# A residual LSTM and RNN over 512 steps: x*Wx0 by seven block products, and a rearranged step

## Chip, cores and metric

One core of a Trainium2 chip runs the whole kernel. The metric is the device time of one execution in microseconds; before the change it is 2285.53 us, the median of three runs (2284.49 to 2286.43).

## What is computed

```python
# first layer, LSTM: x [16, 512, 512], xW = x @ Wx + b, Wx and Wh [512, 2048]
a = xw_t + prev_h @ Wh
i, f, o = sigmoid(a[:, :H]), sigmoid(a[:, H:2*H]), sigmoid(a[:, 2*H:3*H])
g = tanh(a[:, 3*H:])
next_c = f * prev_c + i * g
next_h = o * tanh(next_c)
# x = x + hs;  second layer, RNN: Wx and Wh [512, 512]
h_next = tanh(h @ Wh + xw_t)
# x = x + hs
```

Everything is fp32. Sixteen sequences go through 512 steps; the second layer takes the first one's output plus x, and starts from the same state cond_1024 as the first.

## The kernel before, in words

The 512 steps run one after another on one core, and five engines have a program each, tied by semaphores. There is no planner: the order of each engine's work is written out by hand in its loop over t, and a wait holds back all that is behind it on the same engine.

**Tiles.** A product has the states as the stationary operand, 128 rows (a quarter of the 512 inputs, index k) by 32 columns, and streams the weights past it. The output has only 32 rows, so each 128-row tile of PSUM is filled by four matmuls side by side, one per quarter q of the array (tiles, L175). A "group" below is such a set of four. The gate columns are laid out so that each half of them holds the i, f, o and g columns of one half of the state.

**Recurrent product of layer one** (recurrent0, L206). The weights are held as two fp16 parts, high and low, and so is the state: the stationary tile holds 16 columns of the state's high part and 16 of its low part. One half of the outputs takes 4 k x 2 parts = 8 groups of 256 columns. The groups of output half 0 come first, and before its third k TensorE waits for the second half of the state (h0_ready[1]). Then come the 8 groups of output half 1.

**x*Wx0** (input0, L191) works on a pair of steps at once, so the stationary tile holds 2 steps x 16 sequences. It is fp32 with 512 columns per matmul, 4 k per pair, two k after each step's recurrent product, one or two steps ahead of their use; an fp32 matmul stands in the trace as two records. ScalarE first puts the bias into the bank (bias0, L470), the product adds to it, and ScalarE copies it, times a mask that picks one of the pair's steps and the scale, into the bank of the recurrent product (seed0, L484), which adds to it.

**Layer two** runs LAG = 4 steps behind: input1 (L218, fp32, 128 columns, two k per step) and recurrent1 (L227, fp16, 8 groups of 128 columns, both weight parts added into the same 128 columns), with bias1 and seed1 on ScalarE. All of it is in one bank, rnn_ps.

**A step on VectorE** (loop at L425): transpose of output half 0 (turn0, L350), add of its high and low rows (add0, L356), the same for half 1, the two products of the gates (gate_products, L362), the cell (cell, L367), the state as an fp16 high part (state_high, L378), as fp32 (L379), and as the low part, the difference (state_low, L386). Between these stand the second layer's parts, turn1 (L400), add1 (L404), state1_high and state1_low (L409, L414), and the outputs add_y0 (L394) and add_y1 (L422). **On ScalarE** (loop at L543): seed0 for the next step, seed1, the second layer's tanh (L555), bias0 or bias1, then gates(0), o_half(0), gates(1), tanh_cell(0), o_half(1), tanh_cell(1) (L502 to L515).

**Queues.** SP loads x in chunks of 16 steps, two buffers, and stores the output per 8 steps; before a load it waits until the first layer and x*Wx0 are through with the buffer. GpSimd works only at the start: memsets, an iota, and an all-reduce over the partitions for the largest weight of each layer (L170), on which VectorE's find_scale (L297) waits. The first layer's scale comes before step 0, the second one's at the end of step 0.

## Time and profile before

| what | value |
|---|---|
| median of three runs | 2285.53 us (2284.49 to 2286.43) |
| the profiled execution | 2284.95 us |
| its span, first to last instruction | 2283.1 us |
| mean granted clock of TensorE | 0.993 of full |
| busy in that span, VectorE | 1976.7 us |
| busy in that span, ScalarE | 1644.5 us |
| HBM traffic | 27.62 MB read, 16.78 MB written |

The profiled execution lies inside the three runs' spread. Its busy times are counted once where instructions of an engine overlap. Matmuls are pipelined, so their durations overlap too, and what a group of them costs is read from one start to the next. In a timeline, "idle before" names who ended the wait.

### The profile page before, as it was taken

How to read it: one execution, taken by the hardware profiler on the slowest of the kernel's cores; microseconds unless marked ns; L12 is line 12 of the kernel's file. 1: busy time of each engine (PE TensorE's matmuls, PEld its weight loads, DVE VectorE, ACT ScalarE, POOL GpSimd, SP SyncE). 2: the span in 40 equal slices, each digit the busy share in tenths (PEclk: the TensorE clock that was granted, in tenths of full speed). 3: DMA queues.
4: the chain of work that ended last, by engine and by line, in shares of the span. 5: the costliest groups of instructions: out<-in, count | busy, mean ns of one | idle time of the engine just before them, and what ended most of it. 6: DMA issues, size and time to landing. Idle time of an engine off the chain costs nothing.

```text
span 2283.1 us, 150617 instructions
## 1 busy us (share of the span) xinstructions
PE 2242.1 (98%) x65564; PEld 1617.7 (71%) x65564; DVE 1976.7 (87%) x10283; ACT 1644.5 (72%) x5662; POOL 1.8 (0%) x10
## 2 busy tenths in 40 slices
PE   5999999999999999999999999999999999999997
PEld 2777777777777777777777777777777777777775
DVE  6888888888888888888888888888888888888887
ACT  5777777777777777777777777777777777777775
POOL 0000000000000000000000000000000000000000
PEclk7999999999999999999999999999999999999999
DMA  5000000000000000000000000000000000000000
GB/s 210 18 13 18 23 23 18 14 18 23 23 18 23 13 18 23 23 18 13 18 23 23 18 23 13 18 23 23 18 13 22 19 23 18 23 14 18 23 13 13
DMA packets 16738, 54.03 MB, mean 24 GB/s; under 512 B 2256, under 2 KB 2384, under 8 KB 14800
## 3 DMA queue, kind: packets, MB, share of 16 engines
q1 hardware_dynamic: 16080, 44.41, 5.5%
q8 instruction: 517, 8.47, 1.6%
q14 instruction: 141, 1.16, 0.2%
HBM read 27.62 MB, written 16.78 MB: 19 GB/s over the span
## 4 chain that ended last, share of the span: by engine, by line
PE 97%; DVE 1%; ACT 1%; DMA 1%; issue 0%; SPq 0%; POOL 0%; DVEq 0%; ACTq 0%
PE rec_ps L178 39%; PE in_ps L178 38%; PE rnn_ps L178 20%; DMA wh_sb<-wh 1%; ACT wh_part L480 0%; DVE wh_part L318 0%; DVE largest_slice L277 0%; DVE turned L350 0%; DVE uv L362 0%; DVE h_parts L378 0%; DVE pre_sb L356 0%; ACT wx_sb L468 0%; DVE turned L400 0%; ACT gates_cell L504 0%; ACT rnn_ps L500 0%
## 5 line engine op out<-in xcount | busy, mean ns | idle before, releaser
L178 PE MATMUL in_ps<-wx_sb,x_sb 128*32 128x512 f32 x8192 | 976.4, 594 | 18.4 <-ACT wx_sb L468 18.4
L178 PE MATMUL rec_ps<-wh_part,h_parts 128*32 128x256 f16 x32704 | 988.9, 273 | 5.3 <-DVE h_parts L386 5.3
L178 PEld LDWEIGHTS rec_ps<-wh_part,h_parts 128*32 128x32 f16 x32704 | 867.4, 97 | 13.1 <-issue 8.0
L350 DVE STREAM_TRANSPOSE turned<-rec_ps 128x256 f32<-128x256 f32 x1024 | 461.0, 450 | 196.7 <-PE rec_ps L178 151.5
L178 PEld LDWEIGHTS in_ps<-wx_sb,x_sb 128*32 128x32 f32 x8192 | 259.0, 110 | 327.7 <-issue 319.1
L178 PEld LDWEIGHTS rnn_ps<-wx_sb,y 128*32 128x32 f32 x8192 | 247.0, 110 | 302.5 <-issue 301.0
L490 ACT ACTIVATE rec_ps<-in_ps,mask_scaled 128x256 f32<-128x256 f32 x1022 | 406.6, 435 | 0.4 <-issue 0.2
L178 PE MATMUL rnn_ps<-wh_part,h_parts 128*32 128x128 f16 x16352 | 323.9, 219 | 7.9 <-DVE h_parts L414 7.9
L178 PE MATMUL rnn_ps<-wx_sb,y 128*32 128x128 f32 x8192 | 318.5, 273 | 1.3 <-ACT rnn_ps L500 1.3
L504 ACT ACTIVATE gates_cell<-gate_ps,unscale 128x128 f32<-128x128 f32 x511 | 187.9, 368 | 180.7 <-DVE gate_ps L356 180.7
L500 ACT ACTIVATE rnn_ps<-rnn_ps,mask_scaled 128x128 f32<-128x128 f32 x511 | 174.8, 342 | 188.7 <-DVE turned L400 188.5
L178 PEld LDWEIGHTS rnn_ps<-wh_part,h_parts 128*32 128x32 f16 x16352 | 287.9, 97 | 9.3 <-ACT rnn_ps L500 5.6
L504 ACT ACTIVATE gates_cell<-pre_sb,unscale 128x128 f32<-128x128 f32 x511 | 205.3, 402 | 119.8 <-DVE pre_sb L356 119.8
L509 ACT ACTIVATE o_scaled<-gates_cell 128x32 f32<-128x32 f32 x1024 | 226.7, 221 | 16.3
L362 DVE SCALAR_TENSOR_TENSOR uv<-gates_cell 128x64 f32<-128x64 f32 x1024 | 227.4, 222 | 1.8 <-ACT gates_cell L504 1.3
L367 DVE SCALAR_TENSOR_TENSOR gates_cell<-uv 128x32 f32<-128x32 f32 x1024 | 196.6, 192 | 35.1
L386 DVE TENSOR_TENSOR h_parts<-h_full,h_parts 128x32 f16<-128x32 f32 x1024 | 192.6, 188 | 18.8
L514 ACT ACTIVATE tanh_c_sb<-gates_cell 128x32 f32<-128x32 f32 x512 | 117.5, 229 | 106.5 <-DVE gates_cell L367 106.3
L555 ACT ACTIVATE h_full<-pre,unscale 128x64 f32<-128x64 f32 x511 | 172.3, 337 | 2.3 <-DVE pre L404 2.3
L400 DVE STREAM_TRANSPOSE turned<-rnn_ps 128x128 f32<-128x128 f32 x512 | 162.3, 317 | 12.6 <-PE rnn_ps L178 4.1
L356 DVE TENSOR_TENSOR gate_ps<-turned 128x128 f32<-128x128 f32 x512 | 153.6, 300 | 17.6
L471 ACT ACTIVATE in_ps<-b_sb 128x512 f32<-128x512 f32 x256 | 151.1, 591 | 0.1
(52 smaller groups left out, 1276.0 us busy)
## 6 DMA issues: line engine op xcount, KB each, us to landing
x_sb<-xT SPq DMA_DIRECT2D x32, 512.0 KB, 3.8
yT<-y SPq DMA_DIRECT2D x64, 256.0 KB, 2.0
wh_sb<-wh SPq DMA_DIRECT2D x5, 1024.0 KB, 9.7
wx_sb<-wx SPq DMA_DIRECT2D x5, 1024.0 KB, 14.4
b_sb<-b SPq DMA_DIRECT2D x1, 256.0 KB, 2.7
b_sb<-b SPq DMA_DIRECT2D x1, 64.0 KB, 12.2
h_first<-h0T SPq DMA_DIRECT2D x1, 32.0 KB, 11.6
```

Of the source, the lines that this page charges most:

```text
L178: last = nc.tensor.matmul(out[QUAD * q:QUAD * (q + 1)], states, weights(q), start=False, stop=True, tile_position=(0, QUAD * q), skip_grou ...
L350: nc.vector.transpose(turned0[:, half].rearrange("p b n -> p (b n)"), rec0_ps[t % 2][half][:, 0:COLSH]).then_inc(turned0_done[half], 1)
L356: nc.vector.tensor_tensor(slices(pre0[half]), turned0[:, half, :, 0:BATCH], turned0[:, half, :, BATCH:], ALU.add).then_inc(pre0_done[half], 1)
L362: nc.vector.scalar_tensor_tensor(uv[:, half], gates_cell[:, half, 0:2], 1.0, gates_cell[:, half, 3:5], ALU.add, ALU.mult).then_inc(uv_done ...
L367: nc.vector.scalar_tensor_tensor(gates_cell[:, half, GATES], uv[:, half, 1], 0.5, uv[:, half, 0], ALU.mult, ALU.add).then_inc(cell_done[ha ...
L386: nc.vector.tensor_tensor(h0_parts[:, subs, BATCH:], slices(h0_full[:, cols]), h0_parts[:, subs, 0:BATCH], ALU.subtract).then_inc(h0_ready ...
L400: nc.vector.transpose(turned1[:, :].rearrange("p b n -> p (b n)"), rec1_ps).then_inc(turned1_done, 1)
L490: last = nc.scalar.activation(rec0_ps[t % 2][half][:, 0:COLSH], in0_ps[t // PAIR % 2][:, half * COLSH:(half + 1) * COLSH], ACT.Copy, scale ...
L500: nc.scalar.activation(rec1_ps, in1_ps[s // PAIR % 2], ACT.Copy, scale=own).then_inc(seed1_done, 1)
L504: nc.scalar.activation(gates_cell[:, half, 0:GATES].rearrange("p g n -> p (g n)"), pre0[half], ACT.Tanh, scale=unscale[0][:, :] if t else ...
L509: nc.scalar.activation(o_scaled[:, half], gates_cell[:, half, 2], ACT.Copy, bias=H_SCALE / 2, scale=H_SCALE / 2).then_inc(o_scaled_done[ha ...
L555: nc.scalar.activation(h1_full[:, :], pre1[:, :], ACT.Tanh, scale=unscale[1][:, :] if s > 1 else 1.0).then_inc(h1_full_done, 1)
```

## The change

**x*Wx0 by seven block products.** The unit is now a span of four steps, two pairs. x is cut into a pair (first or second) and a half of k, Wx0 into a half of k and a half of the columns: 2 x 2 blocks times 2 x 2 blocks, eight block products of 2 k by 256 columns. They are replaced by seven over sums of blocks (units). GpSimd forms four sums of the blocks of Wx0 once, at the start (sum_wx0, 2048 columns each), and four sums of the blocks of x per chunk of 16 steps (sum_x, 256 columns each), one at each of the steps 3 to 6 of the chunk before. The first span is done by eight plain block products. The 14 units of a span (7 products x 2 k) are spread over four steps as 4, 3, 4 and 3. Results shared by several blocks are copied on: ScalarE copies v to SBUF (copy_v) and z to c11 (begin_c11), and VectorE adds z and v into c12 (begin_c12) and at the end of the span into c22 (finish_c22); biases go into z and v, each 256 columns wide.

**Layer two's recurrent product** keeps the two weight parts apart: four groups of 256 columns, high and low part side by side. seed1 writes half of the seed into both. Afterwards ScalarE copies the low part's 128 columns to SBUF (copy_low1), VectorE adds the high part's (sum1), and the transpose reads that sum from SBUF. input1 is split into three k and one k over two steps.

**The order.** One group of output half 1 (k = 0, high part) stands before the wait for the state's second half. The second output half has one bank instead of two. On VectorE, sum1, the new adds and turn1 stand ahead of turn0(0); high parts, cells and low parts of the state are reordered; add_y1 stands before state_low(1). On ScalarE, seed0 is issued by half, tanh1 is behind gates(0). find_scale and the weight parts of layer two come two steps later. The start and the loads are adapted.

```diff
+    def sum_x(v, i):
...
+        x = x_sb[:, v % 2].rearrange("p k (g r t) n -> p r k g (t n)", g=PER_CHUNK, r=2)
+        a11, a12, a21, a22 = x[:, 0, 0:SUBH], x[:, 0, SUBH:SUB], x[:, 1, 0:SUBH], x[:, 1, SUBH:SUB]
+        sums = x_sums[:, v % 2]
+        if i == 0:
+            pool.wait_ge(x_in[v % 2], loads(v))
+            if v >= 2:
+                pool.wait_ge(slot_done, slots_until((v - 1) * CHUNK - 6))
+        if i in (1, 3):
+            pool.wait_ge(x_summed, 4 * v + i)
+        out, one, op, other = ((sums[:, 0], a21, ALU.add, a22), (sums[:, 1], sums[:, 0], ALU.subtract, a11),
+                               (sums[:, 2], a11, ALU.subtract, a21), (sums[:, 3], a12, ALU.subtract, sums[:, 1]))[i]
+        nc.gpsimd.tensor_tensor(out, one, other, op).then_inc(x_summed, 1)
...
+    def sum_wx0(i):
+        b11, b12 = wx0_sb[:, 0:SUBH, :, 0:COLSH], wx0_sb[:, 0:SUBH, :, COLSH:COLS]
+        b21, b22 = wx0_sb[:, SUBH:SUB, :, 0:COLSH], wx0_sb[:, SUBH:SUB, :, COLSH:COLS]
+        if i < 2:
+            pool.wait_ge(wx0_doubled, SUBH * (i + 1))
+        if i in (1, 3):
+            pool.wait_ge(wx0_summed, i)
+        one, other = ((b12, b11), (b22, wx0_sums[:, 0]), (b22, b12), (b21, wx0_sums[:, 1]))[i]
+        nc.gpsimd.tensor_tensor(wx0_sums[:, i], one, other, ALU.subtract).then_inc(wx0_summed, 1)
...
+    reduce_largest(0)
+    for i in range(4):
+        sum_wx0(i)
+    reduce_largest(1)
+    for t in range(STEPS):
+        v, c = divmod(t, CHUNK)
+        if 3 <= c < 7 and v + 1 < CHUNKS:
+            pool.wait_ge(rec0_done[0], t + 1)
+            sum_x(v + 1, c - 3)
...
+    def units(g, first, end):
+        z = z_ps[g % 2]
+        products = (
+            (z, lambda k: x_pair(g, 0, k), wx0_block(0, 0)),
+            (v_ps[g % 2], lambda k: x_sum(g, 0, k), wx0_sum(0)),
+            (z, lambda k: x_sum(g, 1, k), wx0_sum(1)),
+            (c11_ps, lambda k: x_pair(g, 0, SUBH + k), wx0_block(1, 0)),
+            (z, lambda k: x_sum(g, 2, k), wx0_sum(2)),
+            (c12_ps, lambda k: x_sum(g, 3, k), wx0_block(1, 1)),
+            (z, lambda k: x_pair(g, 1, SUBH + k), wx0_sum(3)),
+        )
+        sum_of = {1: 0, 2: 1, 4: 2, 5: 3}
+        for u in range(first, end):
+            j, k = divmod(u, 2)
+            if k == 0:
+                if j == 0 and g % PER_CHUNK == 0:
+                    pe.wait_ge(x_in[g // PER_CHUNK % 2], loads(g // PER_CHUNK))
+                if j in sum_of:
+                    sums_ready(g, sum_of[j])
+            out, states, weights = products[j]
+            last = tiles(out, states(k), lambda q: weights(k, q))
+        last.then_inc(slot_done, 1)
...
+    def recurrent0(t):
+        def group(half, k, part):
             cols = slice(half * COLSH, (half + 1) * COLSH)
-            for k in range(SUB):
-                if t and half == 0 and k % SUBH == 0:
-                    pe.wait_ge(h0_ready[k // SUBH], t)
-                for part in weights:
-                    last = tiles(rec0_ps[t % 2][half][:, 0:COLSH], states[:, k], lambda q: part[:, k, q, cols])
-            last.then_inc(rec0_done[half], 1)
+            return tiles(rec0_ps(t, half), h0_parts[:, k], lambda q: wh0_part[part][:, k, q, cols])
+        pe.wait_ge(seed0_done[0], t + 1)
+        pe.wait_ge(h0_ready[0], t)
+        for k in range(SUBH):
+            for part in range(2):
+                group(0, k, part)
+        pe.wait_ge(seed0_done[1], t + 1)
+        group(1, 0, 0)
+        pe.wait_ge(h0_ready[1], t)
+        for k in range(SUBH, SUB):
+            for part in range(2):
+                last = group(0, k, part)
+        last.then_inc(rec0_done[0], 1)
+        for k in range(SUB):
+            for part in range(0 if k else 1, 2):
+                last = group(1, k, part)
+        last.then_inc(rec0_done[1], 1)
...
-        for k in range(half * SUBH, (half + 1) * SUBH):
+        for k in (range(SUB - 1, SUB) if half else range(SUB - 1)):
             last = tiles(in1_ps[r % 2], y0[:, r % Y0_PAIRS, k].rearrange("p t n -> p (t n)"), lambda q: wx1_sb[:, k, q])
...
-    def recurrent1(s, states, weights):
+    def recurrent1(s):
...
         for k in range(SUB):
-            for part in weights:
-                last = tiles(rec1_ps, states[:, k], lambda q: part[:, k, q])
+            if s:
+                last = tiles(rec1_ps, h1_parts[:, k], lambda q: wh1_parts[:, k, q].rearrange("p b w c -> p (b w c)"))
+            else:
+                last = tiles(rec1_by_part[:, :, 0], h_first[:, k], lambda q: wh1_sb[:, k, q])
         last.then_inc(rec1_done, 1)
...
             if t == 1:
                 pe.wait_ge(w_low, 1)
-            recurrent0(t, h0_parts, wh0_part)
-            p, half = divmod(t + 3, PAIR)
-            if p < PAIRS:
-                input0(p, half)
+            recurrent0(t)
+            if t < SLOTS:
+                g, part = divmod(t + 5, SPAN)
+                pe.wait_ge(seed0_done[0], t + 2)
+                if part == 0:
+                    pe.wait_ge(z_biased, g - 1)
+                elif part == 1:
+                    pe.wait_ge(c11_begun, g)
+                elif part == 2:
+                    pe.wait_ge(c12_begun, g)
+                else:
+                    pe.wait_ge(c22_done, g)
+                    if g + 1 < SPANS:
+                        pe.wait_ge(v_biased, g)
+                units(g, UNITS_OF_PART[part], UNITS_OF_PART[part + 1])
         s = t - LAG
         if s >= 0:
...
+    def begin_c12(g, t):
+        dve.wait_ge(slot_done, slots_until(t - 1))
+        dve.wait_ge(v_copied, g)
+        dve.wait_ge(seed0_done[1], t + 1)
+        nc.vector.tensor_tensor(c12_ps, z_ps[g % 2], v_sb[:, :], ALU.add).then_inc(c12_begun, 1)
+    def finish_c22(g, t):
+        dve.wait_ge(slot_done, slots_until(t - 1))
+        if g >= 2:
+            dve.wait_ge(seed0_done[1], SPAN * (g - 1))
+        nc.vector.tensor_tensor(c22_sb[g % 2][:, :], z_ps[g % 2], v_sb[:, :], ALU.add).then_inc(c22_done, 1)
...
+    def sum1(s):
+        dve.wait_ge(rec1_copied, s + 1)
+        nc.vector.tensor_tensor(rec1_sum[:, :, :], rec1_by_part[:, :, 0], rec1_low[:, :, :],
+                                ALU.add).then_inc(rec1_summed, 1)
     def turn1(s):
-        dve.wait_ge(rec1_done, s + 1)
-        nc.vector.transpose(turned1[:, :].rearrange("p b n -> p (b n)"), rec1_ps).then_inc(turned1_done, 1)
+        dve.wait_ge(rec1_summed, s + 1)
...
     for t in range(END):
-        n, s = t + 1, t - LAG
-        lstm, rnn, rnn_state = t < STEPS, 0 <= s < STEPS, s >= 1
-        if lstm:
-            if t == 0:
-                rnn_largest()
-                dve.wait_ge(cell_zeroed, 1)
-            turn0(0, t)
-            add0(0, n)
-            turn0(1, t)
-        if rnn_state:
-            state1_high(s - 1)
-        if lstm:
-            add0(1, n)
-            gate_products(0, n)
-            cell(0, n)
-        if rnn_state:
-            state1_low(s - 1)
-        if lstm:
-            gate_products(1, n)
-            cell(1, n)
-            state_high(0, n)
-        if rnn_state:
-            add_y1(s - 1)
-        if lstm:
-            state_low(0, n)
-            state_high(1, n)
-            state_low(1, n)
+        n, s = t + 1, t - LAG - 1
+        lstm, rnn = t < STEPS, s >= 0
+        g, part = divmod(t + 5, SPAN)
+        if t == 0:
+            rnn_largest()
+            dve.wait_ge(cell_zeroed, 1)
+        if rnn:
+            sum1(s)
+        if lstm and t < SLOTS:
+            if part == 2:
+                begin_c12(g, t)
+            elif part == 3:
+                finish_c22(g, t)
         if rnn:
             turn1(s)
         if lstm:
-            add_y0(t)
+            turn0(0, t)
         if rnn:
             add1(s)
-        if t == 0:
-            find_scale(1, 7)
-        elif t == 1:
+        if lstm:
+            add0(0, n)
+            turn0(1, t)
+            add0(1, n)
+            gate_products(0, n)
+        if rnn:
+            state1_high(s)
+        if lstm:
+            cell(0, n)
+        if rnn:
+            state1_low(s)
+        if lstm:
+            gate_products(1, n)
+            state_high(0, n)
+            cell(1, n)
+            state_full(0, n)
+            state_low(0, n)
+            state_high(1, n)
+            state_full(1, n)
+        if rnn:
+            add_y1(s)
+        if lstm:
+            state_low(1, n)
+            add_y0(t)
+        if t == 2:
+            find_scale(1, done + 1)
+        elif t == 3:
...
+    def bias_z(g):
+        return nc.scalar.activation(z_ps[g % 2], b0_sb[:, 0:COLSH], ACT.Copy)
+    def bias_v(g):
+        return nc.scalar.activation(v_ps[g % 2], b0_diff[:, :], ACT.Copy)
+    def copy_v(g):
+        if g >= 2:
+            act.wait_ge(c22_done, g - 1)
+        nc.scalar.activation(v_sb[:, :], v_ps[g % 2], ACT.Copy).then_inc(v_copied, 1)
+    def begin_c11(g):
+        return nc.scalar.activation(c11_ps, z_ps[g % 2], ACT.Copy)
...
-    def seed0(t):
-        act.wait_ge(in0_done, t // PAIR + 1)
-        if t >= 2:
-            for half in range(HALVES):
-                act.wait_ge(turned0_done[half], t - 1)
+    def seed0(half, t):
+        g, part = divmod(t, SPAN)
+        source = ((c11_ps, c12_ps) if part < PAIR else (z_ps[g % 2], c22_sb[g % 2][:, :]))[half]
+        if half == 0 and t >= 2:
+            act.wait_ge(turned0_done[0], t - 1)
+        if half == 1 and t >= 1:
+            act.wait_ge(turned0_done[1], t)
         own = (mask_scaled[0] if t else mask)[:, t % PAIR:t % PAIR + 1]
-        for half in range(HALVES):
-            last = nc.scalar.activation(rec0_ps[t % 2][half][:, 0:COLSH], in0_ps[t // PAIR % 2][:, half * COLSH:(half + 1) * COLSH],
-                                        ACT.Copy, scale=own)
-        last.then_inc(seed0_done, 1)
+        return nc.scalar.activation(rec0_ps(t, half), source, ACT.Copy, scale=own).then_inc(seed0_done[half], 1)
+    def in1_by_part(i):
+        return in1_ps[i].rearrange("p (b w c) -> p b w c", w=1, c=QUAD).broadcast_to([P, SUB, 2, QUAD])
     def seed1(s):
         act.wait_ge(in1_done, s // PAIR + 1)
         if s:
-            act.wait_ge(turned1_done, s)
-        own = (mask_scaled[1] if s else mask)[:, s % PAIR:s % PAIR + 1]
-        nc.scalar.activation(rec1_ps, in1_ps[s // PAIR % 2], ACT.Copy, scale=own).then_inc(seed1_done, 1)
+            act.wait_ge(rec1_summed, s)
+        own = (mask_scaled[1] if s else mask_half)[:, s % PAIR:s % PAIR + 1]
+        nc.scalar.activation(rec1_by_part, in1_by_part(s // PAIR % 2), ACT.Copy, scale=own).then_inc(seed1_done, 1)
+    def copy_low1(s):
+        act.wait_ge(rec1_done, s + 1)
+        nc.scalar.activation(rec1_low[:, :, :], rec1_by_part[:, :, 1], ACT.Copy).then_inc(rec1_copied, 1)
+    def tanh1(s):
+        act.wait_ge(pre1_done, s + 1)
+        nc.scalar.activation(h1_full[:, :], pre1[:, :], ACT.Tanh,
+                             scale=unscale[1][:, :] if s else 1.0).then_inc(h1_full_done, 1)
...
     for t in range(END):
         s = t - LAG
-        if t + 1 < STEPS:
-            seed0(t + 1)
-        if t == 1:
+        g, part = divmod(t + 5, SPAN)
+        ahead = t < SLOTS
+        if t < STEPS:
+            act.wait_ge(slot_done, slots_until(t - 1))
+            if t:
+                seed0(1, t)
+        if s >= 1:
+            copy_low1(s - 1)
+        if t < STEPS:
+            if t + 1 < STEPS:
+                seed0(0, t + 1)
+            if t == 1:
+                copy_v(1)
+            if part == 0 and g < SPANS:
+                act.wait_ge(seed0_done[0], t + 2)
+                bias_z(g).then_inc(z_biased, 1)
+            elif part == 1 and ahead:
+                act.wait_ge(seed0_done[0], t + 2)
+                if g > 1:
+                    copy_v(g)
+                begin_c11(g).then_inc(c11_begun, 1)
+            elif part == 3 and g + 1 < SPANS:
+                bias_v(g + 1).then_inc(v_biased, 1)
+        if t == 3:
             act.wait_ge(scaled, 2)
             for k in range(SUB):
-                high_part(flat(wh1_sb[:, k]), 1, flat(wh1_part[0][:, k]))
+                high_part(wh1_sb[:, k].rearrange("p q (b c) -> p (q b) c", c=QUAD), 1,
+                          wh1_parts[:, k, :, :, 0].rearrange("p q b c -> p (q b) c"))
         if 0 <= s < STEPS:
             seed1(s)
+        if t < STEPS:
+            gates(0, t)
         if s >= 1:
-            act.wait_ge(pre1_done, s)
-            nc.scalar.activation(h1_full[:, :], pre1[:, :], ACT.Tanh,
-                                 scale=unscale[1][:, :] if s > 1 else 1.0).then_inc(h1_full_done, 1)
-        if t % 2 == 0 and t // 2 + 2 < PAIRS:
-            act.wait_ge(seed0_done, t + 2)
-            bias0(t // 2 + 2)
```

## Rows read from the trace of the kernel before

**Rows 1.** The page, part 1: busy time, share of the span, instructions.

```profile
PE 2242.1 (98%) x65564; PEld 1617.7 (71%) x65564; DVE 1976.7 (87%) x10283; ACT 1644.5 (72%) x5662; POOL 1.8 (0%) x10
```

**Rows 2.** Table by stretch, whole loop: busy per engine, granted clock, DMA share, GB/s.

```profile
100.00:2200.00 2100.00, 2099.96 (x61778) 1521.96 (x61771) 1835.35 (x9653) 1531.76 (x5308) 0.00 (x0) 1.00 0.06 19
```

**Rows 3.** Timeline of TensorE in mid-run: start us, duration us, instruction, [idle before].

```profile
1001.17 0.62 PE L178 MATMUL rnn_ps<-wx_sb,y 128*32 128x128 f32 x16
1001.61 0.63 PE L178 MATMUL rnn_ps<-wh_part,h_parts 128*32 128x128 f16 x32
1002.05 1.94 PE L178 MATMUL rec_ps<-wh_part,h_parts 128*32 128x256 f16 x64
1003.80 1.90 PE L178 MATMUL in_ps<-wx_sb,x_sb 128*32 128x512 f32 x16
1005.51 0.62 PE L178 MATMUL rnn_ps<-wx_sb,y 128*32 128x128 f32 x16
...
1006.40 1.94 PE L178 MATMUL rec_ps<-wh_part,h_parts 128*32 128x256 f16 x64
```

**Rows 4.** Timeline of VectorE and ScalarE, same stretch: two waits.

```profile
1007.50 0.45 DVE L350 STREAM_TRANSPOSE turned<-rec_ps 128x256 f32<-128x256 f32 x1 [0.30 <-PE rec_ps L178]
...
1003.98 0.37 ACT L504 ACTIVATE gates_cell<-gate_ps,unscale 128x128 f32<-128x128 f32 x1 [0.51 <-DVE gate_ps L356]
```

**Rows 5.** Timeline of all engines near the end, steps without x*Wx0.

```profile
2260.08 1.93 PE L178 MATMUL rec_ps<-wh_part,h_parts 128*32 128x256 f16 x64 [0.32 <-DVE h_parts L386]
...
2262.06 0.45 DVE L350 STREAM_TRANSPOSE turned<-rec_ps 128x256 f32<-128x256 f32 x1
...
2262.55 0.29 DVE L356 TENSOR_TENSOR pre_sb<-turned 128x128 f32<-128x128 f32 x1
...
2262.87 0.40 ACT L504 ACTIVATE gates_cell<-pre_sb,unscale 128x128 f32<-128x128 f32 x1 [0.24 <-DVE pre_sb L356]
...
2263.31 0.23 DVE L362 SCALAR_TENSOR_TENSOR uv<-gates_cell 128x64 f32<-128x64 f32 x1
...
2263.57 0.19 DVE L367 SCALAR_TENSOR_TENSOR gates_cell<-uv 128x32 f32<-128x32 f32 x1
...
2263.77 0.18 DVE L379 TENSOR_TENSOR h_full<-o_scaled,gate_ps 128x32 f32<-128x32 f32 x1
2263.79 0.23 ACT L514 ACTIVATE tanh_c_sb<-gates_cell 128x32 f32<-128x32 f32 x1 [0.21 <-DVE gates_cell L367]
...
2264.01 0.18 DVE L386 TENSOR_TENSOR h_parts<-h_full,h_parts 128x32 f16<-128x32 f32 x1
...
2264.23 0.19 DVE L379 TENSOR_TENSOR h_full<-o_scaled,tanh_c_sb 128x32 f32<-128x32 f32 x1
...
2264.34 1.93 PE L178 MATMUL rec_ps<-wh_part,h_parts 128*32 128x256 f16 x64 [0.32 <-DVE h_parts L386]
2264.45 0.19 DVE L386 TENSOR_TENSOR h_parts<-h_full,h_parts 128x32 f16<-128x32 f32 x1
```

**Rows 6.** Timeline of TensorE: step 6, and a second-layer step behind the last state.

```profile
66.36 1.93 PE L178 MATMUL rec_ps<-wh_part,h_parts 128*32 128x256 f16 x64
...
2272.83 0.63 PE L178 MATMUL rnn_ps<-wh_part,h_parts 128*32 128x128 f16 x32 [1.69 <-DVE h_parts L414]
```

**Rows 7.** Groups of instructions by line, whole run: busy us, mean ns, idle before.

```profile
L490 ACT ACTIVATE rec_ps<-in_ps,mask_scaled 128x256 f32<-128x256 f32 x1022 | 406.6, 435 | 0.4 <-issue 0.2
...
L500 ACT ACTIVATE rnn_ps<-rnn_ps,mask_scaled 128x128 f32<-128x128 f32 x511 | 174.8, 342 | 188.7 <-DVE turned L400 188.5
...
L356 DVE TENSOR_TENSOR gate_ps<-turned 128x128 f32<-128x128 f32 x512 | 153.6, 300 | 17.6
```

**Rows 8.** Timeline of GpSimd, first 45 us.

```profile
0.72 0.53 POOL L164 MEMSET zeros<- 128x512 f16 x1 [0.29 <-POOLq L604]
...
11.73 0.13 POOL L167 IOTA partition<- 128x1 int32 x1 [10.25 <-issue]
21.56 0.38 POOL L170 PARTITION_ALL_REDUCE largest_all<-largest  x1 [9.70 <-issue]
38.69 0.35 POOL L170 PARTITION_ALL_REDUCE largest_all<-largest  x1 [16.75 <-DVE largest L277]
```

155 lines of the change are left out of this document (105 added, 50 removed).

## The prediction

> **What bounds the kernel now.** I read the page first: TensorE is busy for 98% of the span, VectorE for 87%, ScalarE for 72% and GpSimd does nothing [rows 1]. Busy shares do not say which of these ends a step, so the next view is the table by stretch: between 100 and 2200 us TensorE is busy all the time and its granted clock is 1.00, the 2.4 GHz level [rows 2]. Then one step of the timeline [rows 3]. From one start of the first layer's recurrent product to the next is 1006.40 - 1002.05 = 4.35 us, and inside it stand 1.75 us of recurrent product, 1.71 us of x*Wx0 (1003.80 to 1005.51), and, a step earlier, 0.44 us of the second layer's input product (1001.17 to 1001.61) and 0.44 us of its recurrent one (to 1002.05). Nothing is left over: a step is TensorE's work. The other engines say the same by waiting: VectorE idles 0.30 us for the product before it transposes, ScalarE 0.51 us before the gates [rows 4].
>
> How far is the next bound? The last steps show it, because there x*Wx0 has run out and TensorE waits 0.32 us for the state. Two recurrent products start 4.26 us apart there (2260.08, 2264.34) [rows 5]. So the chain product, transpose, add, gates, cell, tanh, state takes 4.26 us by itself. **Only 0.09 us of a saving on TensorE would be kept if that chain stayed as it is.** Over the whole loop, step 6 starts at 66.36 us and step 511 at 2264.34: 2197.98 / 505 = 4.352 us a step [rows 5, 6].
>
> **TensorE's new step.** Sixteen groups of four matmuls with 256 fp16 columns take 1.75 us, 0.109 us each. x*Wx0 streams 512 fp32 columns in 4 record groups in 1.71 us, 0.43 us each, so it is paid by the column. Per four steps it had 16 such groups, 6.86 us; seven block products instead of eight leave 7/8 of the columns, plus about 0.03 us for twice as many starts: 6.03 us, 1.51 us a step, 0.43 us for each of the 14 units (one k of one product, two passes of 256 columns). That saves 0.21 us a step. The second layer's recurrent product turns eight groups of 128 columns into four of 256: the same columns, 0.44 us for both; I give it nothing. The input product is split 3 + 1 over two steps instead of 2 + 2, which evens out the 3 and 4 units of x*Wx0 beside it. TensorE's step becomes 4.352 - 0.21 = **4.14 us**.
>
> **The chain's new step.** I count from R, the start of the groups that need the state's second half. Before, 12 groups follow R (1.31 us), then 0.23 us until the transpose of half 1. From that transpose [rows 5]: add +0.49, gates +0.81, products +1.25, cell +1.51, tanh +1.73, second state (L379) +2.17, its low part +2.39 to +2.58, and TensorE starts 0.15 us after a low part is written (64.01 + 0.18 to 64.34). 1.31 + 0.23 + 2.58 + 0.15 = 4.27, and the rows show 4.26: the count holds. Now the moved group: 11 groups follow R, 0.11 us less. VectorE also reaches the second state sooner, since one of the queued operations ahead of it goes: 0.06 us. That path is 4.08 us. The other path goes through the first half: cell 1, then h_full 0, then the low part of half 0 at R + 3.26, written at 3.45, TensorE at 3.60; but now five groups (four and the moved one) stand before the next R: 3.60 + 0.545 = **4.145 us**. So TensorE's work and the chain come out level, and both are 0.21 us shorter than the step now. Whatever delays either is paid in full.
>
> **What is put into the chain.** On VectorE each step now begins with sum1, which waits for ScalarE's copy, which waits for TensorE's last product. TensorE's product ends 0.545 us before R; +0.25 for the wait, +0.30 for the copy (not shown: between 0.23 for 32 columns, L514, and 0.342 for the 128-column activation with a pointer scale [rows 5, 7]; I take it near the latter), so sum1 starts at R + 0.02. It is an add of 128 columns, 0.300 us [rows 7]. Behind it the second layer's transpose, moved from after the state to here, starts at R + 0.36 and lets go of VectorE at 0.60; the first transpose of layer one is due at R + 0.68 and does not wait. Of this 0.00 is on the path. In two steps of four an add of 256 columns (0.300 + 128 more columns, about 0.43) stands between them. In the first (begin_c12) transpose 0 slips to 0.81, add0(0) to 1.29, transpose 1 to 1.50 instead of 1.43: 0.07 us. After that late step sum1 comes 0.07 us early against R, and the second (finish_c22) costs nothing.
>
> On ScalarE the worst step is the one with copy_v and begin_c11: copy_low1 at R - 0.31, seed0 at -0.07, both done at 0.37, copy_v, then begin_c11 ready at about R + 1.15 to 1.24, while TensorE wants it at R + 1.20: 0.03 us late. A seed is 0.435 us [rows 7], and two overlap by 0.07. Behind it seed1, now writing 256 columns, ends its issue at R + 1.45; gates(0) are due at 1.50. bias_z and bias_v take the place of bias0 and hide in the 0.51 us gap [rows 4]. Together 0.10 us in four steps, 0.025 us a step: **4.17 us**.
>
> **GpSimd in the loop** is new: four sums of 256 columns in every 16 steps, each released by rec0_done[0], at R + 0.7. No row shows GpSimd beside VectorE. The bounds: nothing, or all of the delay worked out under the first rival, 0.08 us a step. It could not gain anything, as it only adds work. I take 0.02, nearer to nothing, since it reaches add1 alone and the two transposes read PSUM. That gives **4.19 us** a step.
>
> **Moved or rewired at no cost.** add_y1 now stands between h_full 1 and its low part, in the 0.22 us that this pair waits for each other anyway (2264.23 to 2264.45) [rows 5]. The second half's bank is single now: seed0(1) is issued behind tanh_cell(1), done at R - 0.42, and TensorE wants it at R - 0.11 for the moved group; if that cover went, each 0.1 us would be a step's. SP's wait before an x load changes its semaphore only: the load is issued some 11 steps before its first use and lands in microseconds. The second layer's state must be back for its product at R + 3.15; the chain transpose 1 at 0.36, add1 1.05, tanh1 1.78, state1 low 2.7 is there before. VectorE's queue itself is no bound: its 87% of 2283 us are 3.86 us a step with overlaps counted once, and sum1 and a half of a 256-column add bring about 0.4 more; where this fills the step is inside the path above.
>
> **The start** gets longer. GpSimd shows 10.25 us of issue before its IOTA, 9.70 before the first all-reduce and none before the second [rows 8]: I read this as about 10 us for each change between kinds of operation. tensor_tensor after the all-reduce, the all-reduce again, and the sums after it are three more. The all-reduce would come at about 28 us behind the sums over x instead of at 21.56, then 10 of change to 38; four sums over 2048 columns, at between one and three passes of the memset's rate (0.53 us for 512 columns [rows 8]), 2.1 to 6.3 us each; I take 4.2, because two inputs are read: 55; 10 of change; the second all-reduce at 65, which VectorE awaits at the end of step 2. Step 4 starts near 69.5, step 6 near 78: **+12 us** against 66.36 [rows 6]. If changes cost far less with the loads over, +3; at the dear end +20. **The end**: the steps behind the last state wait only for their own chain (TensorE idles 1.69 us in one [rows 6]), which gains a copy and an add, 0.7 us in each of four: +3 us.
>
> By the Trainium skill (GPSIMD Engine Reference, Performance versus the Vector engine) a tensor_tensor of 2048 fp32 elements takes 4497 ns on GpSimd; with it the start would be +13 instead of +12.
>
> **The sum**: 505 x (4.352 - 4.19) = -82; +12; +3: -67 on a span of 2283.1 gives 2216. The profiled execution took 2284.95, 1.85 us more than its span, and the median of the runs is 0.6 above that: **2218.5 us**, 2.9% faster.
>
> **Rivals.**
> 1. **GpSimd's sum holds VectorE's two-input operations off.** A sum of 256 columns lasts between 0.3 us (one pass at the memset's rate) and 0.94 (three); take 0.62. It starts at R + 0.78 and ends at 1.40. add1, with both inputs in SBUF, could start at 1.05, so add0(0) comes at 1.52, transpose 1 at 1.73 instead of 1.43: 0.30 us in 4 of 16 steps, 0.075 us a step. 4.245: 2247 us. For it: the place is in the chain. Against it: no row. Chance 0.22. The Trainium skill (SBUF — State Buffer, Who interferes with whom) says that a VectorE instruction with two SBUF inputs contends with a GpSimd instruction that reads SBUF; no run here shows it yet.
> 2. **ScalarE's run of copies is late.** If copy_low1, copy_v and begin_c11 each cost 0.1 us more than assumed, c11 is 0.3 us later once in four steps, 0.075 us a step: 2247 us too. Chance 0.15.
> 3. **Nothing added is on the path**: 4.145 us and a start of +7: 505 x 0.207 = 104.5 less 10: 2191 us. Chance 0.12.
> 4. **Slower**: the mechanism of rival 1, with sums that last over 0.93 us. Then each costs over 0.61 us, a step exceeds 4.32, and the 15 us at both ends are no longer covered. At 1.2 us: 0.88 x 4/16 = 0.22, a step of 4.39, 2320 us. The upper bound of a pass count, 0.94, just reaches the point. Chance 0.06.
>
> **Numbers.** The forecast has 0.45. The range takes in rivals 1 to 3 and the ends' bounds (3 to 20 us at the start): 2190 to 2260. A measurement can tell about 0.2%, 4.6 us, from no change. Faster 0.92, same 0.02, slower 0.06.
>
> **What would show it.** Right: recurrent products about 4.17 to 4.19 us apart; x*Wx0 1.51 us of each step; TensorE over 98% busy, or idle only before the recurrent product or before the unit after begin_c11; transposes 1.42 us after R. GpSimd shows two more issue gaps near 10 us before 66 us. Rival 1: add1 longer or later in steps 3 to 6 of every 16. Wrong: steps over 4.3 us, a transpose 0 that waits for sum1 in every step, or x*Wx0 that costs more than 0.43 us per unit of 256 columns.

## The result, and the profile after

The changed kernel takes 2291.20 us (median of 12 runs, 2287.06 to 2296.74) against 2285.62 for the kernel before (12 runs): a ratio of 1.0025, 95% interval 1.0017 to 1.0033. It is slower by a quarter of a per cent, where 2218.5 us were forecast. The profiled execution took 2291.07 us with a span of 2289.3. Part 1 of its page, against [rows 1]:

```profile
PE 2205.7 (96%) x63548; PEld 1838.2 (80%) x63548; DVE 2118.7 (93%) x11050; ACT 1776.5 (78%) x6431; POOL 115.7 (5%) x143
```

TensorE is busy for 36 us less than before, and the span is 6 us longer: the engine now waits. To see where, I take the start of the transpose of half 1 as the mark of a step. In the kernel before the 7th stands at 68.34 us and the 512th at 2266.32, 4.352 us a step; after, at 92.29 and 2268.56, 4.309 a step. So 505 steps gained 21.7 us where 82 were forecast, the way to the 7th grew by 24.0 us where 12 were, and the rest behind the last by 4.0 where 3 was.

**The steps alternate.** The timeline of TensorE after, against [rows 3]:

```profile
1002.65 0.62 PE L244 MATMUL c_ps<-wx_sb,x_sums 128*32 128x256 f32 x8
1003.26 0.43 PE L244 MATMUL rnn_ps<-wx_sb,y 128*32 128x128 f32 x8
...
1006.96 0.87 PE L244 MATMUL rnn_ps<-wx_sb,y 128*32 128x128 f32 x24
1007.61 0.65 PE L244 MATMUL rnn_ps<-wh_parts,h_parts 128*32 128x256 f16 x16
...
1010.69 1.05 PE L244 MATMUL in_ps<-wx_sums,x_sums 128*32 128x256 f32 x16
1011.73 0.43 PE L244 MATMUL rnn_ps<-wx_sb,y 128*32 128x128 f32 x8
```

and of ScalarE in the same stretch:

```profile
1002.41 0.40 ACT L704 ACTIVATE gates_cell<-pre_sb,unscale 128x128 f32<-128x128 f32 x1
1002.76 0.20 ACT L714 ACTIVATE gate_ps<-gates_cell 128x32 f32<-128x32 f32 x1
1002.90 0.26 ACT L663 ACTIVATE rnn_ps<-b_sb 128x128 f32<-128x128 f32 x1
```

The unit that starts at 1002.65 costs 0.43 us everywhere else, but the one quarter of the second layer's input product behind it starts only at 1003.26, 0.61 later. In front of it TensorE's program waits for in1_biased: the bias copy L663 runs at 1002.90 to 1003.16, behind the gates and the tanh of the cell. Two steps later the same (16 records take 1.04 instead of 0.86 before 1011.73). The step between (1006.96) has no such wait. The bias waited for is not that of the quarter part behind it: it is the next pair's, which the three-quarter part reads a step later. The wait stands so early in both kernels; what the change moved is the copy on ScalarE, from in front of gates(0) to behind tanh_cell(0). So odd steps take 4.32 us and even ones 4.15. The table of waits does not name ScalarE for it; it has it as issue time of the weight loads (us in total, times, longest), once in every second step:

```profile
PEld rnn_ps L244 <- issue: 142.2, 272, 2.7
```

**Steps with a sum on GpSimd.** In four steps of every 16 the period is 0.21 us longer. Timelines of GpSimd and VectorE in one of them, and then the same VectorE line in a step without a sum:

```profile
1457.65 0.73 POOL L211 TENSOR_TENSOR x_sums<-x_sb 128x256 f32<-128x256 f32 x1 [55.36 <-PE rec_first_ps L244]
```

```profile
1457.98 0.48 DVE L572 TENSOR_TENSOR pre<-turned 128x64 f32<-128x64 f32 x1
...
1001.23 0.18 DVE L572 TENSOR_TENSOR pre<-turned 128x64 f32<-128x64 f32 x1
```

add1, a 64-column add with both inputs in SBUF, lasts 0.48 us instead of 0.18 and ends at 1458.46, just behind the sum (1458.38). add0 and the transpose of half 1 stand behind it. This is rival 1 of the prediction, in its place and with nearly its size. By the rule that the prediction named with it (the Trainium skill, SBUF — State Buffer, Who interferes with whom), the trace agrees.

**The start.** GpSimd's first 61 us, against [rows 8]:

```profile
1.77 0.14 POOL L192 IOTA partition<- 128x1 int32 x1 [0.29 <-issue]
...
17.34 0.72 POOL L211 TENSOR_TENSOR x_sums<-x_sb,x_sums 128x256 f32<-128x256 f32 x1
26.89 0.38 POOL L195 PARTITION_ALL_REDUCE largest_all<-largest  x1 [8.84 <-issue]
...
35.41 4.60 POOL L222 TENSOR_TENSOR wx_sums<-wx_sb 128x2048 f32<-128x2048 f32 x1 [8.15 <-issue]
...
49.98 4.82 POOL L222 TENSOR_TENSOR wx_sums<-wx_sb,wx_sums 128x2048 f32<-128x2048 f32 x1
...
60.78 0.38 POOL L195 PARTITION_ALL_REDUCE largest_all<-largest  x1 [5.98 <-DVE largest L418]
```

and VectorE beside the four large sums:

```profile
32.42 1.42 DVE L463 SCALAR_TENSOR_TENSOR wh_part<-wh_sb,w_scale,wh_part 128x512 f16<-128x512 f32 x2 [0.33 <-ACT wh_part L669]
34.17 23.83 DVE L463 SCALAR_TENSOR_TENSOR wh_part<-wh_sb,w_scale,wh_part 128x512 f16<-128x512 f32 x10 [0.33 <-ACT wh_part L669]
```

Two low parts of the weights take 1.42 us alone; the next ten take 23.83 instead of some 7. Taken one by one, four of the ten last 5.0 to 5.1 us, each until just behind the end of one of GpSimd's four sums of 4.6 to 5.0 us, and the other six 0.74 us. The changes of GpSimd's kind of operation cost 8.84 and 8.15 us, and the third, in front of the second all-reduce, at most 5.98, where the forecast had about 10 for each. So that all-reduce comes at 60.78, before the 65 of the forecast; late are VectorE's low parts.

**Rare long steps.** Beside the three patterns there are single steps of 4.6 to 5.3 us, in which TensorE's rows fall into pieces of one to four quarters. Above the medians of their place in the 16 they come to about 12 us in the loop (between 1 and 3 before, by how the medians are rounded). What they are is read from the traces behind e14.

The step adds up: 4.15, and 252 x 0.17 / 505 = 0.085 for the bias, 124 x 0.21 / 505 = 0.052 for the sums, 12.3 / 505 = 0.024 for the rare ones: 4.31, measured 4.309. The last term is only what is left over. The experiments take the others away one at a time, then ask what made the 4.15.

### The profile page after: what moved, and what is told of

Read it like the earlier page. It is cut to its first block, busy times and chain, and to the rows that moved or that the text cites. A ratio compares the mean times of both kernels' runs of the same rounds, so it can differ in the third digit from the quotient of the medians.

```text
span 2289.3 us, 148190 instructions
## 1 busy us (share of the span) xinstructions
PE 2205.7 (96%) x63548; PEld 1838.2 (80%) x63548; DVE 2118.7 (93%) x11050; ACT 1776.5 (78%) x6431; POOL 115.7 (5%) x143
## 4 chain that ended last, share of the span: by engine, by line
PE 95%; DVE 2%; issue 1%; ACT 1%; DMA 1%; POOL 0%; SPq 0%; DVEq 0%; ACTq 0%; POOLq 0%
PE in_ps L244 24%; PE rnn_ps L244 22%; PE rec_first_ps L244 20%; PE rec_second_ps L244 19%; PE c_ps L244 10%; DVE wh_part L463 1%; DMA x_sb<-xT 1%; ACT wh_part L669 0%; DVE turned L494 0%; DVE wh_parts L463 0%; POOL x_sums L211 0%; ACT wh_parts L669 0%; DVE largest_slice L418 0%; SPq L162 0%; DVE h_parts L547 0%
## 5 line engine op out<-in xcount | busy, mean ns | idle before, releaser
L244 PE MATMUL rec_second_ps<-wh_part,h_parts 128*32 128x256 f16 x16352 | 661.9, 273 | 0.2 <-issue 0.2
L244 PE MATMUL rec_first_ps<-wh_part,h_parts 128*32 128x256 f16 x16352 | 610.5, 273 | 22.5 <-DVE h_parts L547 20.8
L244 PEld LDWEIGHTS rec_first_ps<-wh_part,h_parts 128*32 128x32 f16 x16352 | 458.9, 97 | 52.9 <-issue 38.5
L244 PEld LDWEIGHTS rec_second_ps<-wh_part,h_parts 128*32 128x32 f16 x16352 | 479.1, 97 | 1.4 <-issue 0.4
L244 PE MATMUL in_ps<-wx_sums,x_sums 128*32 128x256 f32 x6096 | 408.9, 379 | 1.1 <-ACT rec_first_ps L680 0.7
L244 PE MATMUL rnn_ps<-wh_parts,h_parts 128*32 128x256 f16 x8176 | 339.5, 274 | 8.2 <-DVE h_parts L582 8.2
L244 PEld LDWEIGHTS rnn_ps<-wh_parts,h_parts 128*32 128x32 f16 x8176 | 245.4, 97 | 11.4 <-issue 8.5
L494 DVE STREAM_TRANSPOSE turned<-rec_first_ps 128x256 f32<-128x256 f32 x512 | 221.0, 432 | 16.7 <-PE rec_first_ps L244 7.5
L691 ACT ACTIVATE rnn_ps<-rnn_ps,mask_scaled 128x256 f32<-128x256 f32 x511 | 224.9, 440 | 13.8 <-DVE rec_sum L561 2.5
L494 DVE STREAM_TRANSPOSE turned<-rec_second_ps 128x256 f32<-128x256 f32 x512 | 228.7, 447 | 0.7 <-PE rec_second_ps L244 0.7
```

What stands on the lines that cost most here:

```text
L244: last = nc.tensor.matmul(out[QUAD * q:QUAD * (q + 1)], states, weights(q), start=False, stop=True, tile_position=(0, QUAD * q), skip_grou ...
L494: nc.vector.transpose(turned0[:, half].rearrange("p b n -> p (b n)"), rec0_ps(t, half)).then_inc(turned0_done[half], 1)
L691: nc.scalar.activation(rec1_by_part, in1_by_part(s // PAIR % 2), ACT.Copy, scale=own).then_inc(seed1_done, 1)
```

## The experiments

All lines of code are of the changed kernel. A ratio is to the kernel before, from runs on the same chip.

**e1, the bias copy earlier.**

```diff
+                if s >= 0 and s % 2 and s // 2 + 2 < PAIRS:
+                    act.wait_ge(seed1_done, s + 1)
+                    bias1(s // 2 + 2)
                 if t < STEPS:
                     gates(0, t)
...
-                if s >= 0 and s % 2 and s // 2 + 2 < PAIRS:
-                    act.wait_ge(seed1_done, s + 1)
-                    bias1(s // 2 + 2)
```

> bias1 alone goes back in front of gates(0). Theory A (TensorE waits for in1_biased in every odd step of layer two, 0.17 to 0.18 us, because bias1 stands behind tanh_cell(0)): the alternation 4.15 / 4.32 us becomes 4.15 / 4.15 outside the steps with a GpSimd sum, 252 x 0.17 = 43 us less, about 2248 us. Theory B (the odd steps are long because four units of 256 fp32 columns plus one k of the input product cost TensorE more than three plus three): the alternation stays and the time stays near 2291 us. Theory C (the wait goes but the chain through VectorE comes out no shorter than 4.3 us): the wait moves to the recurrent product and less than 15 us are gained.

Measured 2237.05 us, ratio 0.9787 [0.9773, 0.9802]: 54 us less than the changed kernel. Every step is 4.15 us but those with a sum (4.35), and the rare long steps fall to about 3 us. 252 x 0.17 = 43 and the 10 of the rare ones are the 54. The first term is shown.

**e2, the sums over x later in the step**, released by ScalarE's copy of the second layer's low part, so that they run beside other VectorE work.

```diff
-                    pool.wait_ge(rec0_done[0], t + 1)
+                    if t > LAG:
+                        pool.wait_ge(rec1_copied, t - LAG)
+                    else:
+                        pool.wait_ge(rec0_done[0], t + 1)
                     sum_x(v + 1, c - 3)
```

> Each GpSimd sum of x is released by rec1_copied, so that it runs beside sum1 and the transposes, which read at most one operand from SBUF, instead of beside add1. Theory A (add1 with two SBUF inputs is held off by the sum and lasts 0.48 us instead of 0.18): the 124 steps with a sum lose their 0.21 us, 26 us less, about 2265 us, and add1 is 0.18 us in all steps. Rival (any GpSimd work beside the step costs the same, wherever it stands): nothing changes, or the delay comes back at another VectorE instruction with two SBUF inputs, 2285 to 2295 us.

**e3, no sums over x in the loop**: it leaves out the sums after the first 16 steps' and uses the first ones throughout, so its output is not right.

> GpSimd forms the sums over x for the first chunk only and the units of all later chunks read those; so the output lacks the right x*Wx0 from step 16 on. Theory A: the same 26 us as with the sums moved, about 2265 us, and no step with an extra 0.21 us; what is left of steps over 4.4 us is not GpSimd's. If the irregular long steps (4.6 to 5.3 us, some 14 us in all) hang on GpSimd, they go too, and the time is about 2250 us.

e2 took 2266.35 us (0.9920 [0.9903, 0.9936]), e3 2265.59 (0.9911 [0.9896, 0.9926]). Leaving the sums out gains no more than moving them within the step. Both show the alternation of 4.15 and 4.32 in all 16 places, so the 25 us are the collision and not the sums. GpSimd's sum keeps its 0.73 us in e2; what counts is which VectorE operation runs beside it. All 120 sums between 100 us and the end now stand beside sum1 (one input in PSUM, one in SBUF) and the second layer's transpose (one input), and these last 0.29 and 0.31 us beside a sum as without one. Part of the rare long steps stays in both.

**e4, the start's sums on VectorE**: the sums over Wx0 and over the first x go from GpSimd to VectorE, between the weights' low parts, and the all-reduces stay alone on GpSimd.

```diff
-            for i in range(4):
-                sum_x(0, i)
             reduce_largest(0)
-            for i in range(4):
-                sum_wx0(i)
             reduce_largest(1)
...
             for k in range(SUB):
...
+                if k == 1:
+                    for i in range(2):
+                        sum_wx0(i)
```

> b0_diff, the first chunk's sums over x and the four sums over Wx0 are done by VectorE between the low parts, and rnn_largest stands behind step 0; GpSimd does its two all-reduces only. Theory A (the start is 22 us late because the low parts, with two SBUF inputs, are held off by GpSimd's 19 us of sums, and because the all-reduce stands behind the sums over x and one more change of kind): the first transpose of half 1 comes at about 45 us instead of 61.2, 15 to 18 us less, about 2274 us. Rival (the start is bound by TensorE's larger first span and by the scale): 3 to 5 us less.

2267.79 us (0.9921 [0.9906, 0.9935]), 23 us less; the first transpose of half 1 is at 43.82 us instead of 61.19 (39.21 before), the seventh at 75.61 instead of 92.29 (68.34 before). So 17 of the 23 us are the start's; most of the others are fewer rare long steps, which this edit does not touch. 7 us of the longer start stay, and no run isolates them. The same sum takes 2.29 us on VectorE where GpSimd took 4.60 and held VectorE off.

**e5, all three repairs.**

> The three remedies together: bias1 in front of gates(0), GpSimd's sums released by rec1_copied, the start's sums on VectorE. If the three costs are separate, each step is 4.15 us: 75.6 us until the seventh transpose of half 1, 505 x 4.15, 21 us behind the last one, 2 us around the span: 2194 us, 4% below the kernel before. If they hide one another in part (moving one lets another come out), 2205 to 2230 us.

2197.16 us (5 runs, 2195.94 to 2198.09), ratio 0.9612 [0.9598, 0.9625]: 3.9% faster than the kernel before, 94 us below the changed one. Single gains of 54, 25 and 23 us make 102, so they nearly add up (some of each is rare long steps, which can be saved once only). The loop runs at 4.162 us a step, 4.15 in the median of every place. **This version beats both kernels**, and it is the base of the rest.

**e6, the moved group put back** behind the first half's eight groups.

```diff
                 pe.wait_ge(seed0_done[0], t + 1)
...
-                pe.wait_ge(seed0_done[1], t + 1)
-                group(1, 0, 0)
                 pe.wait_ge(h0_ready[1], t)
```

> As e5_all_three, but with the group of the second output half back behind the first half, so 12 groups follow the wait for the state's second half instead of 11. Theory A (work and chain are level at 4.145 us, the chain through half 1 is then 4.08 + 0.11 = 4.19): steps of 4.19 us, about 20 us slower than e5_all_three. Rival (the chain has slack of 0.1 us or more): the same time as e5_all_three.

2196.18 us (0.9608 [0.9594, 0.9621]), 4.159 a step: the moved group is worth nothing.

**e7, the second layer unsplit**: its product as before in eight groups of 128 columns, without copy and sum.

```diff
-                    if s:
-                        last = tiles(rec1_ps, h1_parts[:, k], lambda q: wh1_parts[:, k, q].rearrange("p b w c -> p (b w c)"))
-                    else:
-                        last = tiles(rec1_by_part[:, :, 0], h_first[:, k], lambda q: wh1_sb[:, k, q])
+                    for w in (wh1_part if s else [wh1_sb]):
+                        last = tiles(rec1_ps, (h1_parts if s else h_first)[:, k], lambda q: w[:, k, q])
...
-                    pool.wait_ge(rec0_done[0], t + 1)
+                    if t > LAG:
+                        pool.wait_ge(rec1_done, t - LAG)
```

> As e5_all_three, but layer two's recurrent product as in the kernel before: eight groups of 128 columns into the same columns, no copy_low1 and no sum1. Theory A (the same columns, and the copy and the add are covered): within 10 us of e5_all_three, steps of 4.14 to 4.16 us, and some 3 us less at the end, where the second layer's chain is bare. Rival 1 (eight groups of 128 columns cost TensorE more than four of 256, or its instructions come too fast): steps longer by 0.02 to 0.1 us, 10 to 50 us slower. Rival 2 (sum1 in front of the transpose is on the path): 10 to 20 us faster.

2270.46 us (2261.97 to 2275.01), ratio 0.9929 [0.9909, 0.9949]: 73 us more than e5. The forecast gave the split nothing, and where TensorE runs freely it is worth nothing in fact: 32 quarters of 128 columns take 0.46 us (1004.23 to 1004.69 here) against the 0.44 of [rows 3]. But steps get long without any pattern, 53 us above the medians, and TensorE's rows break up:

```profile
1004.23 0.63 PE L228 MATMUL rnn_ps<-wh_part,h_parts 128*32 128x128 f16 x32
1004.69 0.62 PE L228 MATMUL rec_first_ps<-wh_part,h_parts 128*32 128x256 f16 x16
...
1008.45 0.27 PE L228 MATMUL rnn_ps<-wx_sb,y 128*32 128x128 f32 x2
1008.47 0.30 PE L228 MATMUL rnn_ps<-wh_part,h_parts 128*32 128x128 f16 x4
1008.56 0.27 PE L228 MATMUL rnn_ps<-wx_sb,y 128*32 128x128 f32 x1
1008.57 0.27 PE L228 MATMUL rnn_ps<-wh_part,h_parts 128*32 128x128 f16 x3
```

**e8, fewer units**: four of the 14 units of x*Wx0 in a span are left out, so that TensorE has 3.72 us of work a step and the chain shows.

```diff
-                    last = tiles(out, states(k), lambda q: weights(k, q))
+                    if g == 1 or u not in (1, 5, 8, 12):
+                        last = tiles(out, states(k), lambda q: weights(k, q))
```

> As e5_all_three, but four of the fourteen units of each span are left out, so the output lacks part of x*Wx0; TensorE's work per step falls by 0.43 us to 3.72 us. Theory A (the state's chain by itself is 4.145 us): steps stay at 4.14 to 4.15 us with TensorE waiting about 0.4 us for h_parts. Rival (the chain is shorter and TensorE alone sets the step): steps of 3.8 to 4.1 us.

2194.06 us (2 runs, 0.9599 [0.9581, 0.9616]). With 0.43 us less work a step the kernel gains 3 us. Every step is 4.15, now with TensorE waiting for the first half's state; timeline of VectorE and TensorE:

```profile
1001.81 0.19 DVE L566 TENSOR_TENSOR h_parts<-h_full,h_parts 128x32 f16<-128x32 f32 x1
...
1002.15 0.62 PE L229 MATMUL rec_first_ps<-wh_part,h_parts 128*32 128x256 f16 x16 [0.22 <-DVE h_parts L566]
```

The chain by itself is 4.15 us, and TensorE's work of 4.14 is level with it, as the prediction's count had it. One thing does not fit: without the moved group that count has 4.19.

**e9, sixteen units**: two units of a span done twice, as many columns as eight block products.

```diff
-                    last = tiles(out, states(k), lambda q: weights(k, q))
+                    for _ in range(2 if u in (5, 12) else 1):
+                        last = tiles(out, states(k), lambda q: weights(k, q))
```

> Based on the kernel with the three repairs (e5, 2197 us, a step of 4.15). Two of the 14 units of x*Wx0 in a span are done twice, so TensorE works off 16, as many columns as eight block products have (its results are other ones for it). What the seventh part of the columns is worth. Theory A, TensorE's work and the chain lie level at 4.14 to 4.15 us: half a unit more a step is 0.43/2 = 0.21 us of TensorE that nothing covers, so every step is 4.35 to 4.37 us and the kernel about 2197 + 505 x 0.21 = 2303 us. Rival B, TensorE still had slack that the chain hid: 0.05 to 0.15 us a step less than that, 2230 to 2275 us, with TensorE waiting for nothing and the chain as the bound.

2295.31 us (1.0043 [1.0028, 1.0057]), 4.356 a step against 4.162: 98 us, 0.194 a step. Theory A in the sum, not in the shape: the two more units fall into the steps that had three and have the three-quarter part of the input product too, so steps of 4.56 alternate with 4.15. 4.56 less one unit of 0.43 is 4.13: TensorE's work in these steps, as the prediction had it. The seven products are worth this, and all of it is kept.

**e10, fewer units and no moved group** (the edits of e8 and e6 together).

> The kernel with four of the 14 units of x*Wx0 in a span left out (e8, 2194 us, steps of 4.15 us that are the chain alone, TensorE waiting 0.22 us in each), and in addition the moved group put back behind the first half's sixteen groups. With TensorE slack the chain shows bare. Theory A, the count of the prediction: the path through the second half had 0.11 us less by the moved group, 4.08; without it that path is 4.19 and sets the step: +0.04 us, 2214 us. Rival B: the step is set by the path through the first half, over which the moved group stands as a fifth group; without it that path gets 0.11 us shorter, and the step falls to between 4.04 and 4.12: 2140 to 2180 us. Rival C: the group is in neither path that decides (what decides is VectorE's or ScalarE's own queue): 4.15 us, 2192 to 2197 us.

2192.66 us (0.9594 [0.9580, 0.9608]), 4.150 a step. Rival C: the group is not in what decides, even with the chain bare. The timelines say why. (The first half has eight groups; the sixteen that the expectation names are the whole product.) In e8 and in e10 the transpose of half 1 starts 1.98 us after the first of the 16 groups (1002.15 and 1004.13; 1001.87 and 1003.85): TensorE works off all 16 from the first half's state on, in whatever order, and from that transpose the way goes back to the first half's low part. The second half's state has to be there only by the fifth group in e10, the sixth in e8, and it is. In e10:

```profile
1002.04 0.18 DVE L565 TENSOR_TENSOR h_parts<-h_full,h_parts 128x32 f16<-128x32 f32 x1
```

```profile
1001.87 1.06 PE L229 MATMUL rec_first_ps<-wh_part,h_parts 128*32 128x256 f16 x32 [0.21 <-DVE h_parts L565]
```

The low part is written at 1002.22 and the fifth group starts at 1002.31, without a gap behind the fourth. The prediction's count put 0.15 us between a low part and TensorE here too; it had read them where TensorE stood still. R was not the point to count from.

**e11, the second layer unsplit and fewer units** (the edits of e7 and e8).

> The kernel with the second layer's product in eight groups of 128 columns again, without copy and sum (e7, 2270 us with irregular steps), and four of the 14 units of x*Wx0 in a span left out: 132 matrix instructions a step instead of 140, and 0.43 us a step less of TensorE's work. Theory S, the irregular steps of e7 come from more instructions than TensorE is brought in the time of a step: 132 come in 4.0 to 4.1 us at the rate of e7's regular steps (140 in 4.21), so the steps are even and the chain sets them, 4.08 to 4.15 us: 2160 to 2197 us, irregular excess under 10 us. Rival T, the irregularity is the chain's own jitter in a kernel without copy and sum: it stays at 30 us or more, 2220 us and over. Of the copy and the sum it tells too: at 4.15 us as in e8 they are not on the path, below it they are.

2246.20 us (0.9829 [0.9814, 0.9843]). The even steps of theory S are there (3.0 us above the medians, 4.15 in 12 places of 16), but the time is above its range; it lies in the range of theory T, though not for its reason, because the four places with a sum on GpSimd take 4.56. Without a copy to wait for, the sum is released by the product itself, earlier, and meets VectorE on the state; timelines of GpSimd and VectorE:

```profile
1082.35 0.73 POOL L210 TENSOR_TENSOR x_sums<-x_sb 128x256 f32<-128x256 f32 x1 [54.61 <-PE rnn_ps L228]
```

```profile
1082.29 0.19 DVE L550 TENSOR_TENSOR h_parts<-o_scaled,tanh_c_sb 128x32 f16<-128x32 f32 x1
1082.39 0.73 DVE L555 TENSOR_TENSOR h_full<-o_scaled,tanh_c_sb 128x32 f32<-128x32 f32 x1
```

32 columns take 0.73 us instead of 0.18; 0.41 of it is paid in each of 124 steps, 51 us, which is the whole gap to 2195. At 4.15 without copy and sum, these two are not on the path.

e7 has the sums in the same place of the program, so part of its 73 us could be this collision. Its trace says no: steps with a sum take 4.32 us in the mean and the others 4.32, and no operation of VectorE is longer beside a sum. In 95 of 120 cases there the sum came while VectorE was already at work on two SBUF inputs, and it was the sum that took longer, 0.81 us instead of 0.73; VectorE, then GpSimd:

```profile
1031.38 0.18 DVE L561 TENSOR_TENSOR h_parts<-h_full,h_parts 128x32 f16<-128x32 f32 x1
1031.48 0.22 DVE L569 SCALAR_TENSOR_TENSOR y<-h_full,x_sb 128x64 f32<-128x64 f32 x1
```

```profile
1031.47 0.82 POOL L210 TENSOR_TENSOR x_sums<-x_sums,x_sb 128x256 f32<-128x256 f32 x1 [3.71 <-PE rnn_ps L228]
```

So e7's 73 us are its irregular steps.

**e12, halved units**: the split stays; 8 of 14 units are done as two products of 128 columns, 140 matrix instructions a step as in e7.

```diff
+                    if u % 2 or u == 6:
+                        last = tiles(out[:, 0:COLSH // 2], states(k), lambda q: weights(k, q)[:, 0:COLSH // 2])
+                        last = tiles(out[:, COLSH // 2:COLSH], states(k), lambda q: weights(k, q)[:, COLSH // 2:COLSH])
...
```

> The kernel with the three repairs (e5, 2197 us), with 8 of the 14 units of x*Wx0 in a span done as two products of 128 columns each instead of one of 256: the same columns and the same results, 16 matrix instructions more a step, 140 instead of 124, as many as in e7. Theory S, the number of matrix instructions in a step is what broke e7 (140 a step do not come evenly in 4.15 us): irregular steps come back, 20 to 60 us above the medians in all, 2235 to 2290 us. Rival T, in e7 it was the second layer's own short groups or the missing copy and sum that broke the rhythm: steps stay at 4.15 to 4.18 us with under 10 us of irregular excess, 2197 to 2212 us.

2300.85 us (2294.4 to 2306.46), ratio 1.0066 [1.0045, 1.0086]. The same columns and the same results cost 104 us, more than theory S allowed. The medians rise too (4.15 to 4.46), and about 40 us lie above them.

**e13, VectorE's order as before** in the middle of a step.

```diff
                     gate_products(1, n)
-                    state_high(0, n)
                     cell(1, n)
+                    state_high(0, n)
                     state_full(0, n)
+                if rnn:
+                    add_y1(s)
+                if lstm:
                     state_low(0, n)
                     state_high(1, n)
                     state_full(1, n)
-                if rnn:
-                    add_y1(s)
-                if lstm:
                     state_low(1, n)
```

> The kernel with the three repairs (e5, 2197 us, steps of 4.15 to 4.16), with VectorE's order in the middle of a step set back to that of before: the first half's rounded state behind the second half's cell instead of before it, and the second layer's output add ahead of the first half's low part instead of behind the second half's state. Theory A: the chain by itself is 4.15 us instead of the 4.26 of the last steps of before because of these two moves alone, which run by the first half's state (full state 0.09 us earlier, low part 0.11 us earlier against the start of the recurrent product). Set back, every step is 4.26 us, TensorE waits for the state in each, and the kernel takes 2197 + 505 x 0.10 = 2248 us (2240 to 2256). Rival B: the order is covered and the chain got shorter by something else (the second layer's transpose moved away from between the steps, the seed by halves, the single bank): 2195 to 2205 us.

2250.33 us (0.9844 [0.9830, 0.9859]), every place 4.26 us (one 4.25). VectorE in that version, then in e8:

```profile
1006.23 0.19 DVE L543 SCALAR_TENSOR_TENSOR gates_cell<-uv 128x32 f32<-128x32 f32 x1
1006.34 0.18 DVE L553 TENSOR_TENSOR h_parts<-o_scaled,gate_ps 128x32 f16<-128x32 f32 x1
1006.44 0.18 DVE L558 TENSOR_TENSOR h_full<-o_scaled,gate_ps 128x32 f32<-128x32 f32 x1
...
1006.53 0.22 DVE L608 TENSOR_TENSOR y<-y,h_full 128x64 f32<-128x64 f32 x1
...
1006.67 0.18 DVE L565 TENSOR_TENSOR h_parts<-h_full,h_parts 128x32 f16<-128x32 f32 x1
```

```profile
1001.38 0.19 DVE L554 TENSOR_TENSOR h_parts<-o_scaled,gate_ps 128x32 f16<-128x32 f32 x1
1001.49 0.19 DVE L544 SCALAR_TENSOR_TENSOR gates_cell<-uv 128x32 f32<-128x32 f32 x1
1001.60 0.18 DVE L559 TENSOR_TENSOR h_full<-o_scaled,gate_ps 128x32 f32<-128x32 f32 x1
```

From the second cell to the first half's low part it is 0.44 us in e13 (1006.23 to 1006.67) and 0.32 in e8 (1001.49 to 1001.81). These two moves in VectorE's order, to which the prediction gave no gain of their own (it has add_y1 under "Moved or rewired at no cost"), are worth 53 us: without them nearly all of TensorE's saving would have stayed behind the 4.26 us of [rows 5].

**e14, fewer units and the second half's groups halved**: much slack by columns (3.72 us a step as in e8), 148 matrix instructions a step.

```diff
...
+                    for lo in (0, COLSH // 2):
+                        last = tiles(rec0_ps(t, half)[:, lo:lo + COLSH // 2], h0_parts[:, k],
+                                     lambda q: wh0_part[part][:, k, q, COLSH + lo:COLSH + lo + COLSH // 2])
```

> The kernel with four of 14 units of x*Wx0 left out (e8, 2194 us, 116 matrix instructions and 3.72 us of TensorE's work a step, steps of 4.15 us set by the chain), with the second half's eight groups of 256 columns done as sixteen of 128: the same columns, 148 instructions a step. Theory S, TensorE is not brought more than about one matrix instruction in 30.5 to 31.2 ns in the long run (140 in 4.317 us in e7, 140 in 4.366 in e12): 148 need 4.51 to 4.62 us, though TensorE has 0.43 us of slack by its columns; the kernel takes 2194 + 505 x (0.36 to 0.47) = 2376 to 2431 us. Rival T, the broken steps of e7 and e12 came from having no slack in the columns, so that any jitter is paid: here the slack covers it, steps stay at 4.15 to 4.18 us, 2194 to 2212 us.

2407.58 us (1.0533 [1.0515, 1.0551]), 214 us more than e8 with the same columns. Theory S, inside its range. The chain did not get longer by the short groups: 187 of the 505 steps still take under 4.2 us, and the others up to 6.6. The table of busy time between 100 and 2150 us, one row each of e5, e8, e7, e12 and e14 (columns: TensorE's matmuls, its weight loads, VectorE, ScalarE, GpSimd, clock, DMA share, GB/s):

```profile
100.00:2150.00 2050.00, 2049.34 (x61096) 1731.72 (x61092) 1974.33 (x10596) 1720.38 (x6160) 87.87 (x120) 1.00 0.06 20
```

```profile
100.00:2150.00 2050.00, 1941.44 (x57292) 1546.15 (x57286) 1963.80 (x10620) 1683.63 (x6170) 88.07 (x120) 1.00 0.06 20
```

```profile
100.00:2150.00 2050.00, 2027.80 (x66502) 1779.59 (x66498) 1785.23 (x9738) 1501.56 (x5462) 95.27 (x120) 1.00 0.06 20
```

```profile
100.00:2150.00 2050.00, 2012.55 (x65731) 1856.72 (x65728) 1885.23 (x10097) 1646.70 (x5870) 85.18 (x116) 1.00 0.06 20
```

```profile
100.00:2150.00 2050.00, 1830.16 (x66481) 1496.45 (x66475) 1798.70 (x9655) 1552.96 (x5615) 82.25 (x112) 1.00 0.06 19
```

Divide 2050 us by the matmuls: 33.6 ns each in e5, 35.8 in e8, and 30.8, 31.2 and 30.8 in e7, e12 and e14. The three broken kernels do different work at different slack and end at the same number: **one matmul with its weight load in about 31 ns, in the long run**. In e14 TensorE is idle for 11% of the stretch and the loop is still longer. Short bursts go faster (e7's 32 in 0.46 us are 14 ns each), so a piece of timeline does not show this bound; the count over milliseconds does. The kernel before had 34.0 ns (2100 us for 61778 [rows 2]), and the changed one 34.8 (2050 us for 58951). e11, with 132 a step, is even at 4.15 us (31.4 ns).

**What the pauses are.** The traces have a DMA queue whose kind is called instruction; its line (packets, MB, share) in e5, then in e14:

```profile
q8 instruction: 503, 8.24, 1.6%
```

```profile
q8 instruction: 599, 9.81, 1.8%
```

A packet has 16 KB, and there is one for every 256 instructions of TensorE in both (128894 and 153534, weight loads, matmuls and waits). Number TensorE's instructions from the first on, and each has a place from 0 to 255 within 256. Between 150 and 2100 us, every pause of over 0.65 us between two matmul starts ends at the places 193 to 196: 17 in e7, 38 in e12, 181 in e14, 4 in the changed kernel.

In e14 nine of ten of them end 1.24 to 1.54 us after a packet of that queue has landed. What the gaps at this place have above the mean gap comes, in the 505 steps, to 71 us in e7, 97 in e12 and 275 in e14 (where TensorE's slack takes part of it), against 5 in e5 and 1 in the kernel before. A step has about 252 of TensorE's instructions in e5, 284 in e7 and 300 in e14, so no place in the step keeps a distance of 256. So the pauses are TensorE without its next packet of instructions, and they account for e7's 73 us and nearly all of e12's 104. In the three broken kernels such a packet comes every 3.9 us, which for some 126 matmuls is the 31 ns. In the changed kernel the same place has 11 us, and each of its 16 steps over 4.6 us has a pause there: these are its rare long steps (3 us in e1). What keeps the packets from coming faster, these runs don't tell.

## Why the prediction was wrong

It said 2218.5 us, faster with 0.92, range 2190 to 2260. The measurement is 73 us above the number and 31 above the range. 505 x (4.309 - 4.19) = 60, 12 at the start, 1 behind the end. In a step the terms are 0.085 for the bias, 0.032 for the sums beyond the 0.02, 0.024 for the rare long steps, 0.005 for the chain, and 0.025 too much for copies and adds: 0.12 together.

- **The steps that failed.** *"bias_z and bias_v take the place of bias0 and hide"*: they do, but the same passage never asked where bias1 had gone. It had moved behind tanh_cell(0), while TensorE's wait for it stayed where it was, a step ahead of the product that reads the bias. A wait of TensorE of 0.17 us in every second step: 43 us, and 54 with the irregular steps that went with it (e1). It is the largest term and had none in the sum.
- **GpSimd in the loop, mis-sized**: I took 0.02 us a step; it is 0.052 (e2, e3). The mechanism of rival 1 was written down with its operation, add1, and a sum of 0.62 us (0.73 measured), and 0.30 us for each (0.21; by its own count, which goes by the end of the sum, one of 0.73 us would have cost 0.41, so that 0.30 came so near is partly luck). It had 0.22, and should have been the forecast: the reason against it was only that no row showed it.
- **The start, mis-sized**: +12, measured +22 at the first transpose and +24 at the seventh. The prices were fair but for the third change (changes of kind 8.8, 8.2 and at most 6.0 us for 10, sums of 4.6 to 5.0 us for 4.2), and GpSimd was done earlier than forecast. What failed is that I let VectorE's low parts run beside the sums, after having written under rival 1 that such operations hold each other off: 23.83 us for ten of them. e4 takes 17 of the 24 back; 7 stay unexplained. One rule was applied in the loop and forgotten in the start. The Trainium skill's figure for such a sum (GPSIMD Engine Reference, Performance versus the Vector engine), 4497 ns, is 2% under the first one's 4.60 us and 9% under the third's 4.96.
- **The layer-two split, "I give it nothing"**: right for the columns (0.44 us either way), wrong for the kernel. Undone, it costs 73 us (e7), because 140 matmuls a step are more than come in 4.15 us at 31 ns (4.34). As the split was part of the change, this did not make the prediction wrong; without it the change would most likely have been slower still, which no run of the unrepaired kernel shows. Seven products of 256 columns raise the count by 12 a step, and the split takes 16 away.
- **The chain**: 4.145 us, measured 4.15 (e8), but for a half-wrong reason. The 0.11 us of the moved group are nothing (e6, e10): without it the count has 4.19 for the path through the second half, and the step stays 4.15. The 4.145 came from the path through the first half, which does not change with the group's place. The gain against 4.26 is VectorE's order (e13), which my count by times carried in the line "cell 1, then h_full 0" without my seeing that it was the gain.
- **Copies and adds in the chain, 0.025 us a step** (begin_c12, begin_c11): nothing; every place of e5 has 4.15. Rival 2 did not happen in its place either. This error is 13 us the other way.
- **Right**: TensorE's work 4.14 (e9: 0.194 us a step for the seventh of x*Wx0, 0.21 forecast); copy and sum off the path (e11); the two bounds level, so that "whatever delays either is paid in full". This is what then happened: 0.17 and 0.21 us delays were paid in full.
- **The reading of TensorE's instructions** had no term at all. The rare long steps of the changed kernel, 12 us, are pauses at the place of a new instruction packet (11 us). Why they shrink with the wait for the bias (3 us in e1) and e5 still has 5 is not isolated.
- Rival 4 (slower by the sums alone) did not happen; it went slower because three terms came together (the bias wait, the sums in the loop, the start), and only the last two were on my list.

## What to carry to other kernels

When TensorE's work and the dependency chain are level, list every producer on the other engines' queues, also the ones that the change only reorders, and ask for each where the wait for it stands, which can be earlier than its first consumer: the 0.26 us bias copy in the wrong place cost more than either new kind of work. Place GpSimd's elementwise work beside VectorE operations that have slack or one SBUF input, and keep it out of a start in which VectorE works on two inputs. Count matmuls per step beside columns, and where TensorE pauses without a releaser, look whether the pauses keep a distance of 256 of its instructions: a change that saves columns by making more, shorter matmuls can lose all of it, and one that merges them can win without saving a column.

## What the runs showed of the hardware

- Matmuls with their weight loads pass at about 31 ns each over milliseconds (30.8, 31.2, 30.8 in three kernels), though bursts of 32 run at 14 ns; at the limit TensorE's rows break into small pieces and steps lose their rhythm.
- TensorE's instructions come in 16 KB packets of 256 (queue q8: 503 packets in e5, 599 in e14). All 236 pauses of over 0.65 us in e7, e12 and e14 end at one place, within four instructions, of the 256.
- A GpSimd sum of 256 columns (0.73 us) makes a VectorE operation with two SBUF inputs that starts behind it last until about the sum's end: 0.48 us instead of 0.18 for 64 columns, 0.73 for 32 (e11), and about 5.0 instead of 0.74 beside the sums of 2048 columns. An add with one input in PSUM and a transpose are not longer (0.29 and 0.31 us, e2). Where VectorE was first, the sum took 0.81 instead of 0.73 (e7).
- A change between GpSimd's elementwise sums and its all-reduce cost 8.84 and 8.15 us of issue, a third at most 5.98. Between the IOTA and the first sum there was none to see (2.07 us, until ScalarE had the bias), and the IOTA that waited 10.25 us before [rows 8] waits 0.29 in the changed kernel.
